# A transformer block on one core: weight blocks divided one turn further ahead, with seven raw buffers, and a first stage that rounds by conversion

## The reference, cut to what matters

```python
x = x + matmul(fake_quant(ln(x)), fake_quant(ctx))       # clip(round(v / s + z), 0, 255)
def block_qdq_weight(w):       # 1376 x 512, blocks of 32 along a row, 4 bits
    scale = max(max(abs(wb)) / 7, 1e-12)
    return clip(round(wb / scale), -8, 7) * scale
def act_qdq(x):                # 16 bits, range over the whole tensor
    scale = (max(x, 0) - min(x, 0)) / 65535
    return (clip(round(x / scale) + zp, 0, 65535) - zp) * scale
xq = act_qdq(ln(x)); up = act_qdq(xq @ wu.T); gate = act_qdq(xq @ wg.T)
o = act_qdq(act_qdq(gate * fixed_qdq(sigmoid(gate))) * up)
x = x + o @ wd.T
```

## Time and profile before

| | |
|---|---|
| runs, median (lowest to highest) | 826.1 us (825.26 to 829.15), 3 runs |
| profiled execution, its time and span | 826.9 us, 825.1 us |
| mean granted clock of TensorE | 0.943 |
| busy PE, DVE, ACT, POOL | 709.1, 645.9, 516.8, 528.8 us |
| chain that ended last: PE, POOL, DVE, issue, DMA, ACT | 64%, 10%, 10%, 5%, 5%, 4% |

### The profile page before, as it was taken

How to read it: one execution, slowest core, us unless ns; L and a number is a source line. 1 busy time by engine, 2 the same in 40 slices (tenths; PEclk the granted TensorE clock), 3 DMA queues, 4 the chain that set the end, 5 groups by cost and what they waited for, 6 DMA issues and landing times.

```text
span 825.1 us, 12740 instructions
## 1 busy us (share of the span) xinstructions
PE 709.1 (86%) x3310; PEld 326.0 (40%) x3311; DVE 645.9 (78%) x1332; ACT 516.8 (63%) x968; POOL 528.8 (64%) x498
## 2 busy tenths in 40 slices
PE   0597989663195997999999999999999688999998
PEld 0243434221032443444444444444444253444443
DVE  6886768878699587888888988888888767656655
ACT  4567757659466446777777777777776543655540
POOL 1897768937376456888788888888884414344330
PEclk9899989975598998999999999999999999999998
DMA  8315665523335236677666666666645612232311
GB/s 321 102 65 121 134 154 118 126 63 76 65 64 128 76 102 134 166 182 183 154 145 132 137 146 143 145 144 143 144 94 102 103 39 86 105 114 78 114 38 51
DMA packets 199348, 97.72 MB, mean 118 GB/s; under 512 B 188929, under 2 KB 189185, under 8 KB 196370
## 3 DMA queue, kind: packets, MB, share of 16 engines
q1 hardware_dynamic: 199314, 97.32, 48.5%
HBM read 49.85 MB, written 1.05 MB: 62 GB/s over the span
## 4 chain that ended last, share of the span: by engine, by line
PE 64%; POOL 10%; DVE 10%; issue 5%; DMA 5%; ACT 4%; SPq 1%; DVEq 0%; ACTq 0%; POOLq 0%
PE ps L998 21%; PE ps L999 20%; PE ps L1000 20%; ACT arena L692 2%; DMA arena<-arena 2%; POOL arena L483 2%; POOL arena L504 2%; DVE arena L1319 2%; DMA arena<-in_ctx_t 2%; DVE arena L1313 2%; DVE arena L1316 2%; PE ps L1164 1%; POOL arena L496 1%; POOL arena L479 1%; POOL arena L473 1%
## 5 line engine op out<-in xcount | busy, mean ns | idle before, releaser
L998 PE MATMUL ps<-arena 128*128 128x512 f16 (+2 forms) x996 | 385.9, 388 | 48.0 <-ACT arena L692 17.7
L999 PE MATMUL ps<-arena 128*128 128x512 f16 (+2 forms) x996 | 385.4, 387 | 0.0
L1000 PE MATMUL ps<-arena 128*128 128x512 f16 (+2 forms) x996 | 384.1, 386 | 0.0
L692 ACT ACTIVATE arena<-arena 128x512 f16<-128x512 f32 (+8 forms) x425 | 279.6, 688 | 99.7 <-POOL arena L649 29.5
L998 PEld LDWEIGHTS ps<-arena 128*128 128x128 f16 (+1 forms) x996 | 99.5, 100 | 175.9 <-issue 55.0
L1000 PEld LDWEIGHTS ps<-arena 128*128 128x128 f16 (+1 forms) x996 | 99.7, 100 | 122.4 <-issue 11.1
L1313 DVE TENSOR_TENSOR arena<-arena 128x512 f16<-128x512 f32 (+1 forms) x169 | 127.7, 786 | 25.0 <-ACT arena L692 24.2
L999 PEld LDWEIGHTS ps<-arena 128*128 128x128 f16 (+1 forms) x996 | 99.4, 100 | 113.0 <-issue 8.4
L649 POOL TENSOR_SCALAR arena<-arena,rden 128x512 f32<-128x512 f32 x128 | 115.0, 898 | 24.2 <-DVE rden L1664 15.0
L1319 DVE SCALAR_TENSOR_TENSOR arena<-ps,arena 128x512 f32<-128x512 f32 (+1 forms) x149 | 100.4, 706 | 15.3 <-ACT arena L692 7.9
L894 ACT ACTIVATE arena<-arena,mneg 128x512 f32<-128x512 f32 x124 | 88.8, 716 | 35.6 <-DVE mneg L1644 35.6
(11 more groups left out here) (125 smaller groups left out, 665.7 us busy)
## 6 DMA issues: line engine op xcount, KB each, us to landing
arena<-in_moe_w SPq DMA_DIRECT2D x18, 768.0 KB, 4.4
arena<-in_ffn_w SPq DMA_DIRECT2D x33, 256.0 KB, 2.8
arena<-in_wq SPq DMA_DIRECT2D x8, 1024.0 KB, 5.2
arena<-in_wo SPq DMA_DIRECT2D x8, 1024.0 KB, 5.0
arena<-in_kv_w SPq DMA_DIRECT2D x4, 1024.0 KB, 4.8
arena<-arena SPq DMA_TRANSPOSE x177, 3.2
arena<-in_ctx SPq DMA_DIRECT2D x1, 2048.0 KB, 9.1
arena<-in_ctx_t SPq DMA_DIRECT2D x1, 2048.0 KB, 13.5
```

Of the source, the lines that this page charges most:

```text
L692: return a.activation(out_, in_, ACT.Copy, scale=scale, bias=bias)
L998: pe.matmul(out_, lhs[0], rhs[0], start=first, stop=False)
L999: pe.matmul(out_, lhs[0], rhs[1], start=False, stop=False)
L1000: return pe.matmul(out_, lhs[1], rhs[0], start=False, stop=last)
```

## The change

It has three parts. (1) Raw buffers go from 5 to 7, the scales' ring from 6 to 8, the high/low ring from 4 to 3; two raw loads are in flight (one semaphore for even blocks, one for odd ones); maxima, division and rounding of a block come one turn earlier; in a DVE turn the extrema of a finished tile now stand ahead of weight_low. (2) In the first stage the magic constant is replaced by writing int32 and clipping, ACT does the lower clip of the context with Relu, the copies of the transposed q1 move ahead of three quarters of the context's split, the row terms are added later (a constant per row, which the norm takes out; the FFN's sum waits for them), the second rstd stands ahead of two kw_low on POOL, and the hidden rows are quantised tile by tile. (3) spread(0) comes after three value units in place of four, and units 7 and 8 come behind the first and the second up tile.

The diff, with the buffers' addresses and the mere renamings cut:

```diff
@@ -39,15 +39,15 @@
-RAW = 5
-DQ = 4
+RAW = 7
+DQ = 3
 SB = 4
...
 ER = 3
-SC = 6
+SC = 8
@@ -327,11 +329,11 @@
-                if not isinstance(n, int) or n >= 1:
-                    sp_wait(in_raw, n * 16)
-                if not isinstance(n, int) or n >= RAW:
-                    sp_wait(w_deq, n - RAW + 1)
-                sp.dma_start(one(raw, n % RAW), one(ffn_w, n)).then_inc(in_raw, 16)
+                if n >= 2:
+                    sp.wait_ge(in_raw[n % 2], 16 * (n // 2))
+                if n >= RAW:
+                    sp.wait_ge(w_deq, n - RAW + 1)
+                sp.dma_start(raws[n % RAW], ffn_w[:, n]).then_inc(in_raw[n % 2], 16)
@@ -351,10 +353,7 @@
             kw_load(2)
-            for n in range(2):
-                turn_w(n)
-                ring(n + RAW + 1)
-            for n in range(2, NCH):
+            for n in range(NCH):
                 turn_w(n)
@@ -513,8 +512,8 @@
                     scale_back(n + 3)
-                if n + 4 < NCH:
-                    divide(n + 4)
+                if n + 5 < NCH:
+                    divide(n + 5)
@@ -538,9 +537,11 @@
                 ct_low(k)
-            for k in range(KD):
-                kw_low(0, k)
+            kw_low(0, 0)
+            kw_low(0, 1)
             rstd(1)
+            kw_low(0, 2)
+            kw_low(0, 3)
             divide(0)
@@ -557,17 +558,18 @@
             v_low(4)
+            divide(3)
             v_low(5)
...
             scale_back(2)
-            for u in range(MT - 1, MT + 1):
-                v_low(u)
-            divide(3)
+            divide(4)
...
                 kw_scale(2, k)
+                if k < 2:
+                    v_low(MT - 1 + k)
                 if k < KD - 1:
@@ -696,12 +698,21 @@
                 half = ctx_raw[:, b * KD:(b + 1) * KD]
-                a.activation(half, half, ACT.Identity, bias=par[:, 3:4], scale=pc[:, 1:2]).then_inc(ctx_scaled, 1)
+                a.activation(ctx_int[:, b * KD:(b + 1) * KD], half, ACT.Relu, bias=par[:, 3:4],
+                             scale=pc[:, 1:2]).then_inc(ctx_scaled, 1)
+            def q1_turned():
+                for k in range(KD):
+                    a.wait_ge(q1t_ps, k + 1)
+                    copy(q1t[:, k], bank(k).bitcast(BF16)[:, 0:TOK]).then_inc(q1t_ready, 1)
             a.wait_ge(in_ctt, 16)
...
                 copy(ct[0][:, k], ctx_t_raw[:, k]).then_inc(ct_hi, 1)
+                if k == 0:
+                    q1_turned()
@@ -710,13 +721,11 @@
-            for k in range(KD):
-                a.wait_ge(q1t_ps, k + 1)
-                copy(q1t[:, k], bank(k).bitcast(BF16)[:, 0:TOK]).then_inc(q1t_ready, 1)
             kw_high(0)
-            a.wait_ge(row_terms, 1)
-            for t in range(NT):
-                a.wait_ge(col_added, t + 1)
+            def row_terms_in(t):
+                a.wait_ge(ext_ready, 1)
                 a.activation(xres[:, t], xres[:, t], ACT.Identity, bias=rsum[:, t:t + 1], scale=1.0).then_inc(row_added, 1)
@@ -781,14 +790,15 @@
             v_out(3)
+            for t in range(NT):
+                row_terms_in(t)
             v_out(4)
...
             v_out(5)
-            v_out(6)
             hidden_high(0, 1.0)
             weight_high(1)
-            v_out(MT - 1)
-            v_out(MT)
+            round_weights(3)
+            v_out(6)
@@ -797,11 +807,14 @@
                 weight_high(n + 2)
-                round_weights(n + 3)
+                if n + 4 < NCH:
+                    round_weights(n + 4)
                 tile_out(n, dst)
...
                 tile_turn(n, up)
+                if n < 2:
+                    v_out(MT - 1 + n)
                 if n >= 4 and n % 2 == 0:
@@ -827,8 +840,8 @@
                     weight_high(2 * FT + i + 2)
-                if i < FT - 3:
-                    round_weights(2 * FT + i + 3)
+                if i < FT - 4:
+                    round_weights(2 * FT + i + 4)
                 u = i // 2
@@ -1033,11 +1046,12 @@
             def hidden_transposes(n):
-                pe.wait_ge(xn_ready, n + 1)
-                for k in range(KD):
-                    for t in range(NT):
+                for t in range(NT):
+                    pe.wait_ge(xn_ready, t + 1)
+                    for k in range(KD):
                         mm = pe.transpose(hidden_bank(n, k)[:, t * P:(t + 1) * P], xn[:, t, k * P:(k + 1) * P], ident[:, :])
-                    mm.then_inc(xt_ps, 1)
+                        if t == NT - 1:
+                            mm.then_inc(xt_ps, 1)
@@ -1063,14 +1077,13 @@
             pe.wait_ge(row_terms, 1)
-            for u in range(4):
+            for u in range(3):
                 v_unit(u)
             spread(0)
-            for u in range(4, MT - 1):
+            for u in range(3, 6):
                 v_unit(u)
             hidden_transposes(0)
-            v_unit(MT - 1)
-            v_unit(MT)
+            v_unit(6)
@@ -1086,6 +1099,8 @@
                 tile(0, i, i % 2)
+                if i < 2:
+                    v_unit(MT - 1 + i)
             for j in range(1, FT // 2):
@@ -1341,8 +1356,8 @@
             def block_maxima(n):
-                v.wait_ge(in_raw, 16 * (n + 1))
-                src = one(raw, n % RAW).rearrange("p (a b) -> p a b", b=QB)
+                v.wait_ge(in_raw[n % 2], 16 * (n // 2 + 1))
+                src = raws[n % RAW].rearrange("p (a b) -> p a b", b=QB)
                 return own.mark(v.tensor_reduce(one(dsc, n % SC), src, AX.X, ALU.max, apply_absolute_value=True))
@@ -1371,18 +1386,12 @@
             own.wait(own.n)
-            own.link(ts(flat(xn), flat(xn), par[:, 2:3], ALU.add, MAGIC, ALU.add))
-            own.link(ts(flat(xn), flat(xn), MAGIC, ALU.max, MAGIC + 255.0, ALU.min))
-            ts(flat(q1), flat(xn), MAGIC + 128.0, ALU.subtract).then_inc(q1_ready, 1)
+            own.link(ts(flat(xn_int), flat(xn), par[:, 2:3], ALU.add, 0.0, ALU.max))
+            ts(flat(q1), flat(xn_int), 255.0, ALU.min, 128.0, ALU.subtract).then_inc(q1_ready, 1)
             for b in range(B):
-                half = flat(ctx_raw[:, b * KD:(b + 1) * KD])
                 v.wait_ge(ctx_scaled, b + 1)
-                own.mark(ts(half, half, MAGIC, ALU.add, MAGIC, ALU.max))
-            own.wait(own.n)
-            for b in range(B):
-                half = flat(ctx_raw[:, b * KD:(b + 1) * KD])
-                ts(flat(q2[:, b * KD:(b + 1) * KD]), half, MAGIC + 255.0, ALU.min, MAGIC + 128.0, ALU.subtract)\
-                    .then_inc(q2_ready, 1)
+                ts(flat(q2[:, b * KD:(b + 1) * KD]), flat(ctx_int[:, b * KD:(b + 1) * KD]), 255.0, ALU.min, 128.0,
+                   ALU.subtract).then_inc(q2_ready, 1)
@@ -1392,7 +1401,7 @@
             for t in range(NT):
-                v.wait_ge(row_added, t + 1)
+                v.wait_ge(col_added, t + 1)
                 v.wait_ge(x1_ps, t + 1)
@@ -1440,20 +1446,14 @@
                 own.link(ts(z, z, MAGIC + QMAX, ALU.min, MAGIC, ALU.subtract))
-                if k == 0:
-                    own.link(ts(lo, z, -1.0, ALU.mult, MAGIC, ALU.add))
-                    ts(hi, lo, QMAX, ALU.add).then_inc(par_ready, 1)
-                else:
-                    ts(hi, z, -1.0, ALU.mult, QMAX, ALU.add).then_inc(par_ready, 1)
+                ts(hi, z, -1.0, ALU.mult, QMAX, ALU.add).then_inc(par_ready, 1)
                 v.wait_ge(par_ready, k + 1)
-            def clip(dst, k):
-                return ts(dst, dst, aqp[:, k, 1:2], ALU.max, aqp[:, k, 2:3], ALU.min)
             parameters(0, NT, 1.0)
-            own.link(ts(flat(xn), flat(xn), aqp[:, 0, 0:1], ALU.mult, MAGIC, ALU.add))
-            own.link(clip(flat(xn), 0))
-            ts(flat(xn), flat(xn), MAGIC, ALU.subtract, SINT, ALU.mult).then_inc(xn_ready, 1)
+            for t in range(NT):
+                own.link(ts(xn_int[:, t], xn[:, t], aqp[:, 0, 0:1], ALU.mult, aqp[:, 0, 2:3], ALU.min))
+                ts(xn[:, t], xn_int[:, t], SINT, ALU.mult).then_inc(xn_ready, 1)
@@ -1474,17 +1474,16 @@
-                if n + 6 < NCH:
-                    block_maxima(n + 6)
+                if n + 7 < NCH:
+                    block_maxima(n + 7)
+                if between:
+                    between()
                 if n + 2 < NCH and low_owner(n + 2) == 1:
                     weight_low(n + 2)
-                if between:
-                    between()
-                if n + 6 < NCH and (n % 2 or n + 6 == NCH - 1):
-                    pair_scales(n + 6)
+                if n + 7 < NCH and (n % 2 == 0 or n + 7 == NCH - 1):
+                    pair_scales(n + 7)
             def integer(dst, src, k):
                 return ts(dst, src, aqp[:, k, 0:1], ALU.mult, aqp[:, k, 2:3], ALU.min)
@@ -1510,6 +1509,7 @@
             pair_scales(5)
+            block_maxima(6)
             with_tiles(0, up_after)
@@ -1586,6 +1586,7 @@
                 v.wait_ge(d_ps, t + 1)
+                v.wait_ge(row_added, t + 1)
```

21 lines of the change are left out of this document (10 added, 11 removed).

## The result

| | before | after |
|---|---|---|
| median (lowest to highest) of 9 runs each, us | 826.21 (824.32 to 829.43) | 822.38 (820.16 to 823.41) |
| ratio, 95% interval | | 0.9943 [0.9926, 0.9961] |
| profiled execution: span, mean granted clock | 825.1, 0.943 | 819.9, 0.949 |
| busy PE, DVE, ACT, POOL, us | 709.1, 645.9, 516.8, 528.8 | 706.3, 648.7, 514.3, 527.8 |

What follows compares the result with a forecast made beforehand. PE was taken as the bound only in the up stage, elsewhere waiting mostly for DVE's extrema before spreads, with POOL pacing the gate stage. +1.7 - 5.1 - 3.6 - 3.4 = -10.4 took 826.1 to 815.7 us; range 809 to 822.

Steps and rivals of the forecast that it cites:

- Start: Start of the value units after the first stage: no change taken, with bounds of -1.9 and +1.0 us.
- Integers at the float rate: DVE's int32 passes: taken at the float pass's 1.29 us, up to twice that, with +1.0 us for the other end.
- rival 3: DVE's passes block POOL, 0.45 us each, 15 us in all: slower, 831 us; chance 0.04.
- First tile: First up tile at 66.1, 3.6 us earlier, after 4.9 idle; one unit at low clock, +2.4; net +1.2 us.
- From up to gate, -5.1: Before the gate stage, PE's 2.68 us wait for extrema and the 2.4 us low clock behind it go: -5.1 us.
- the prediction's own signs of being wrong: POOL's gate-stage mean rises, PE waits for weights' transfers in the up stage, or stages after 303 us change length.
- Gate stage, -3.6 and full clock: With extrema ahead, only tiles 9 and 10 remain behind DVE's weight_low(23): -3.6 us more; the stage starts at full clock.
- Sigmoid stage, -3.4: ACT loses one rounding (1.3), waits for divide (1.1) and part of its k_low waits (1.0): -3.4 us, between -1.2 and -5.8.
- Rival 2: Look-ahead buys nothing: gate stage restarts at low clock, DVE catches up no earlier, sigmoid gives 1.2; 823.9 us, chance 0.14.
- Rival 1: Earlier start carries: clock kept before the first tile (2.4), units 1.9 earlier, sigmoid 1.8 more; 809.6 us, chance 0.18.

Runs made afterwards that it cites:

- k2: The changed kernel with the hidden rows quantised in two passes of 2048 in place of eight of 512; median 820.13 us, ratio 0.9922.
- m2: The changed kernel with useless matmuls in PE's gaps, 18 ahead of the first up tile and 4 in each gap at the second spread; median 820.29 us.
- k9: The changed kernel run once more, unedited; median 822.52 us, ratio 0.9951.
- k10: The kernel before with part 1 of the change, but weight_low kept ahead of the extrema in a DVE turn; median 819.88 us, ratio 0.9908.
- k1: The kernel before with one edit, the extrema of the finished tile ahead of weight_low in a DVE turn; median 823.88 us, ratio 0.9965.
- k5: The kernel before with part 1 of the change alone, DVE's order included; first stage and value units as before; median 819.98 us, ratio 0.9915.
- k8: The change with two hidden-row passes, weight_low(0) early, block 4-5 maxima and scales early, scale_back(2) and divide(4) before v_low(6), last four kw scalings on ACT; 815.13 us.
- k4: The changed kernel with value units 7 and 8, their copies and low halves back ahead of the first up tiles; median 820.29 us, ratio 0.9940.

## Why the prediction was wrong

Three steps failed: the eight integer passes, priced by their columns and called hidden; the way from the up to the gate stage, where the wait and the low clock were to go; and the gate stage, where the look-ahead was put at nothing and the order at 3.6. By its own steps, in the two profiles of the change:

- **Start: 0 taken, -1.95 and -1.45 measured**; the lower end of its bounds. Over all profiles it is less: the thirteen with this start begin at 36.0 on average, the four with the old one at 37.2. POOL's first subtractions fell from 3.23 to 2.13 us, the four scalings from 4.30 to 2.38.
- **"Integers at the float rate": a step that failed.** The rate was right (1.29 without company; 2.13 and 1.88 for the two passes of k2 beside POOL). The cut into eight was not priced: each of them took 1.15 to 1.38, where a quarter of 1.29 is 0.32 and its other end, twice that, 0.65. The prediction named the Trainium skill's rule of the port pair for the start and for rival 3, and not here. So what was to be hidden behind PE's three units came out as waits (0.76 and 1.82): the transposes ended 25.1 us behind the first unit, where 21.4 (58.6 less 37.2) was forecast. Of these 3.7 us some 0.8 are the spread, which took 2.2 us for 1.4. In k2, with two passes, the transposes wait for nothing and end 21.5 us behind its first unit.
- **First tile: mechanism right, not its time.** Gap of 4.14 for 4.9 and a low clock for one tile behind it, as said, and m2 shows that it is worth something. In k9 the clock fell sooner, behind the transposes' waits (0.67 from 60.36 to 64.30), and the gap was 2.50. The tile came 31.8 and 31.1 us behind the first unit for 28.9, by the integers above.
- **From up to gate, -5.1: the second step that failed.** The wait went from 2.68 to 0.94 (1.06 in k9) and the low clock stayed (0.65, k9 again); about 1.7 of 5.1 came. The stretch from the first up tile to the second spread also held two waits for weights, 0.86 and 0.69, where 0.5 was allowed; that PE waits for these transfers was one of the prediction's own signs of being wrong. From first unit to second spread 76.0 was forecast and 80.5 and 79.6 came: 4.0 us too few.
- **Gate stage, -3.6 and full clock.** 48.5 was forecast, 51.0 and 50.9 came, 49.5 with the gaps filled: 1.5 of the miss is the clock. Of the reason given, DVE's order, k10 shows nothing at the end. The look-ahead, put at nothing ("POOL is never idle", "DVE's wait for a load, behind PE's own time: nothing beyond the above"), is the part that k1 and k5 show: -4.1 us of time between them, some of it the clock's. The earlier trace rows begin at 138.8; over the whole gate stage of the kernel before POOL was busy 41.4 of 54.5 us and waited 9.3 of them for ACT. That the last tiles have less behind the last weight_low came true (4.7 us for 7.6), but that weight_low itself came 1.0 us later, at 161.87.
- **Sigmoid stage, -3.4: -1.5 and -1.3 came.** The rounding (1.3) went. ACT's waits did not: for POOL they were 3.7 us before (2.4 in two, 1.1 in three, 0.2 in one) and are 3.5 in five after, the ones for divide as before (1.0 in three):

```profile
ACT arena L694 <- POOL arena L532: 1.8, 1, 1.8
ACT arena L694 <- POOL arena L495: 1.0, 3, 0.5
ACT arena L694 <- POOL rk L528: 0.7, 1, 0.7
```

Too little came in the three stages, by 4.0, 2.5 and 2.0 us (the mean of the two profiles), and 1.7 more than forecast at the start: 6.8 at the fourth spread, where the median has 6.6, the difference between 10.4 and 3.8. **Rival 2** came nearest (823.9): right on the low clock and on the sigmoid stage, wrong that DVE would catch up no earlier, by the same 4.7 us for 7.6. **Rival 3** did not come: POOL's mean from 138.8 to 165 stayed 1.05 us. **Rival 1** asked for a kept clock behind the first gap, which k8 had (a gap of 2.04, a clock of 1.00) and the change did not.

The parts don't add up to the change. By the medians, -6.3 for part 1 and -3.8 for the first stage with two passes make -10.1, 6.3 more than came. If costs simply add, k2 puts the eight passes at 2.3 of these and m2 the low clock at 2.1; but k5 had a low stretch of its own, and each of these figures is uncertain by about 2 us. 1.9 stay unassigned, among them part 3, of which k4 bounds the place of value units 7 and 8 loosely and no run has the earlier spread(0).
